# A multi-adapter linear layer and a mixture of low-rank experts: one index load, the bias sum on 64 partitions, and another order of the loads

## The reference

```python
# first layer, with one adapter pair per sequence, chosen by an index out of 32 slots
c = x @ W.T + b + 2.0 * (x @ A[idx]) @ Bm[idx]
# second layer
base = c @ W_base.T + b_base
logits = c @ W_router.T                    # 8 experts
rw, sel = top_k(logits, 2); rw = softmax(rw)
w = einsum('tk,tke->te', rw, one_hot(sel)) # weights of the experts per token
h = einsum('td,erd->ter', c, A_experts)    # rank 16 per expert
out = x + base + 2.0 * einsum('ter,te,eor->to', h, w, B_experts)
```

## Time and profile before

| | us |
|---|---|
| median of 3 runs | 67.73 |
| lowest and highest run | 66.97, 67.77 |
| the profiled execution's own time | 67.57 |
| its span | 65.8 |

### The profile page before, as it was taken

The page is one execution under the profiler, slowest core; times in us unless marked ns, Lnnn a source line. Parts: engine busy times, 40 slices in busy tenths (PEclk is TensorE's granted clock), DMA queues, the critical chain, the costliest instruction groups (busy, mean ns, idle before and its releaser), DMA issues.

```text
span 65.8 us, 1181 instructions
## 1 busy us (share of the span) xinstructions
PE 61.9 (94%) x424; PEld 60.8 (92%) x424; DVE 35.9 (55%) x103; ACT 21.5 (33%) x46; POOL 17.0 (26%) x30
## 2 busy tenths in 40 slices
PE   5999979999999999999999999999999999999930
PEld 5979879999999999998999999999999999999920
DVE  0056289998599667015935495002668363857320
ACT  0660358905989399127104100010201040020000
POOL 6810000000699982695390000010100000000000
PEclk9999999999999999999999999999999999999999
DMA  0899998219999004245559999700044000013532
GB/s 0 247 376 259 393 411 262 71 54 175 217 356 369 25 0 101 60 104 129 123 136 339 275 283 401 267 15 0 0 159 159 10 0 0 0 66 123 215 146 87
DMA packets 5865, 10.55 MB, mean 160 GB/s; under 512 B 731, under 2 KB 2523, under 8 KB 5860
## 3 DMA queue, kind: packets, MB, share of 16 engines
q1 hardware_dynamic: 5570, 10.15, 48.0%
q10 hardware_dynamic: 290, 0.33, 1.5%
HBM read 7.37 MB, written 2.10 MB: 144 GB/s over the span
## 4 chain that ended last, share of the span: by engine, by line
PE 83%; DMA 9%; SPq 1%; ACT 1%; DVE 1%; issue 1%
PE ps L661 26%; PE ps L673 19%; PE ps L567 17%; DMA wt<-w_chunks 9%; PE ps L721 9%; PE ps L628 5%; PE ps L696 2%; PE ps L701 2%; PE ps L684 1%; PE ps L707 1%; SPq L223 1%; ACT wt_hi L330 1%; PE ps L639 1%; DVE xn L520 1%
## 5 line engine op out<-in xcount | busy, mean ns | idle before, releaser
L661 PE MATMUL ps<-am,x_hi 128*128 128x384 f32 x64 | 16.6, 340 | 0.0
L673 PE MATMUL ps<-bm,x_hi 128*128 128x280 f32 x64 | 13.0, 297 | 0.0
L661 PEld LDWEIGHTS ps<-am,x_hi 128*128 128x128 f32 x64 | 11.4, 188 | 0.0
L661 PE MATMUL ps<-am,x_lo 128*128 128x384 f32 x32 | 10.8, 338 | 0.0
L297 POOL TENSOR_TENSOR x_lo<-xt,x_hi 128x512 fp32r<-128x512 f32 x8 | 10.8, 1367 | 0.0
L673 PEld LDWEIGHTS ps<-bm,x_hi 128*128 128x128 f32 x64 | 10.2, 188 | 0.0
L673 PE MATMUL ps<-bm,x_lo 128*128 128x280 f32 x32 | 9.3, 291 | 0.0
L567 PE MATMUL ps<-wt_hi 128*128 128x280 f32 (+1 forms) x32 | 7.4, 327 | 0.5 <-ACT wt_hi L330 0.3
L520 DVE TENSOR_TENSOR xn<-ps,xn 128x280 f32<-128x280 f32 (+1 forms) x16 | 6.1, 418 | 2.4 <-PE ps L721 2.3
L567 PE MATMUL ps<-wt_lo,wt_hi 128*128 128x280 f32 (+1 forms) x32 | 7.0, 316 | 0.0
L567 PE MATMUL ps<-wt_hi,wt_lo 128*128 128x280 f32 (+1 forms) x32 | 6.5, 310 | 0.0
(11 more groups left out here) (70 smaller groups left out, 98.5 us busy)
## 6 DMA issues: line engine op xcount, KB each, us to landing
xt<-x_t SPq DMA_DIRECT2D x4, 512.0 KB, 6.5
xn<-x_n SPq DMA_DIRECT2D x4, 512.0 KB, 6.0
out_n<-xn SPq DMA_DIRECT2D x7, 256.0 KB, 2.0
wt<-w_chunks SPq DMA_DIRECT2D x3, 582.0 KB, 6.6
g_st<-g_hl SPq DMA_DIRECT2D x12, 81.0 KB, 2.1
ab<-adapters SPq DMA_DIRECT2D x8, 64.0 KB, 2.7
wt<-w_chunks SPq DMA_DIRECT2D x2, 128.0 KB, 2.9
btt<-b_t SPq DMA_DIRECT2D x1, 256.0 KB, 5.0
```

The source lines that it names most:

```text
L661: last = mm(a_bank(b)[:, 0:R + WA], v[:, p, i, tok], am[:, i, level, at:at + R + WA], start=(i == 0 and n == 0), stop=False, skip_group_ch ...
L673: mm(b_bank(b)[:, 0:QB], v[:, p, i, tok], bm[:, i, level, :], start=(i == 0 and n == 0), stop=False, skip_group_check=True)
```

## The change

- `bsum` is not cleared, and `b_base` is not put into it. Its first step is a scaled copy of chunk 0's columns on ScalarE; VectorE adds the chunks 1 to 3.
- VectorE copies partitions 64 to 127 of `bsum` into a scratch that is the later `hw`, and adds them to partitions 0 to 63. ScalarE rounds these into the lower half of `bsum_st`; VectorE writes the low part into the upper half. `C` is then one matmul over 128 rows for each column range.
- `b_base` is the last of the loads, into one partition of the scratch. It is rounded into high and low parts of its own (`bb_hl`), which become two more rows of `g_st`: `GK` is 100 instead of 98, and `slots_routed(0)` waits for four spread rows instead of two.
- SP issues chunks 1 to 3 one after the other, then loads all eight indices with one call, then the adapters, then x's first pair and the rest.
- ScalarE rounds the adapters before x's first pair. POOL starts its series after `bsum_lo_done` instead of `bs_lo_done`. VectorE takes the low part of the bias sum before it reads `M` out.

The core of the diff:

```diff
-GK = CROW + 2
+GK = CROW + 4
...
+        bsum_st = sb("bsum_st", [P, WC], F32R)
+        cb_hl = sb("cb_hl", [HP + 1, 2, WC], F32R)
+        c_hl, bb_hl = cb_hl[0:1], cb_hl[HP:HP + 1]
...
+        hw_flat = hw[:].rearrange("p a t c -> p (a t c)")
+        upper, bb = hw_flat[0:HP, 0:WC], hw_flat[HP:HP + 1, 0:WC]
...
                 sp.dma_start(wt[:, k, :], w[:, k, :]).then_inc(w_in[k], 16)
-                if k == 1:
-                    sp.wait_ge(bsum_zero, 1)
-                    sp.dma_start(bsum[0:1, :], bbase).then_inc(bbase_in, 16)
-            sp.dma_start(xt[:, 0], x[:, 0]).then_inc(x_in[0], 16)
-
             sp.wait_ge(idx_in, 16)
-            for b in range(NB):
-                slot = sp.value_load(idx_sb[0:1, b:b + 1], min_val=0, max_val=SLOTS - 1)
+            _, slots = nc.values_load_multi_w_load_instructions(
+                idx_sb[0:1, :], engines=[mybir.EngineType.SP], min_val=0, max_val=SLOTS - 1)
+            for b, slot in enumerate(slots):
                 sp.dma_start(ab[:, b].rearrange("p c k r -> p (c k r)"),
...
+            sp.dma_start(xt[:, 0], x[:, 0]).then_inc(x_in[0], 16)
             sp.dma_start(xt[:, 1], x[:, 1]).then_inc(x_in[1], 16)
...
                 sp.dma_start(xt[:, p], x[:, p]).then_inc(x_in[p], 16)
+            sp.dma_start(bb, bbase).then_inc(bbase_in, 16)
+
+            def spread(row, src):
+                sp.dma_start(g_st[row:row + 1, :, :].bitcast(F32),
+                             src.bitcast(F32).to_broadcast([1, PAIRS, WC])).then_inc(cst_in, 16)
+
+            sp.wait_ge(bb_hi_done, 1)
+            spread(CROW, bb_hl[:, 0:1, :])
+            sp.wait_ge(bb_lo_done, 1)
+            spread(CROW + 1, bb_hl[:, 1:2, :])
...
-            nc.gpsimd.memset(bsum[:], 0.0).then_inc(bsum_zero, 1)
...
-            pool.wait_ge(bs_lo_done, 1)
+            pool.wait_ge(bsum_lo_done, 1)
             pool.wait_ge(ab_hi_done, 2)
...
+            act.wait_ge(w0_in[2], 16)
+            nc.scalar.activation(bsum[:], wt[:, 0, D:CH], ACT.Copy,
+                                 scale=wt[:, 0, CH:CH + 1]).then_inc(bsum_first, 1)
...
-            x_high(0)
             act.wait_ge(ab_in, 16 * NB)
             hi(bs_hi[:].rearrange("p k b r -> p b k r"), ab[:, :, 1]).then_inc(ab_hi_done, 1)
             hi(as_hl[:, :, :, 0, :], ab[:, :, 0]).then_inc(ab_hi_done, 1)
-            act.wait_ge(bsum_done, KB)
-            hi(bsum_hl[:, 0], bsum[:]).then_inc(bsum_hi_done, 1)
-
+            x_high(0)
+            act.wait_ge(halves_done, 1)
+            hi(bsum_st[0:HP], bsum[0:HP]).then_inc(bsum_hi_done, 1)
             for i in range(KB):
...
+            act.wait_ge(bbase_in, 16)
+            hi(bb_hl[:, 0], bb).then_inc(bb_hi_done, 1)
             x_high(1)
...
-                if k == 1:
-                    dve.wait_ge(bbase_in, 16)
-                bias_sum(k - 1)
+                if k > 1:
+                    bias_sum(k - 1)
             bias_sum(KB - 1)
+            dve.wait_ge(bsum_done, KB - 1)
+            nc.vector.tensor_copy(upper, bsum[HP:P]).then_inc(upper_done, 1)
+            dve.wait_ge(upper_done, 1)
+            nc.vector.tensor_tensor(bsum[0:HP], bsum[0:HP], upper, ALU.add).then_inc(halves_done, 1)
             dve.wait_ge(ab_hi_done, 1)
             lo(bs_lo[:].rearrange("p k b r -> p b k r"), ab[:, :, 1],
                bs_hi[:].rearrange("p k b r -> p b k r")).then_inc(bs_lo_done, 1)
+            dve.wait_ge(bsum_hi_done, 1)
+            lo(bsum_st[HP:P], bsum[0:HP], bsum_st[0:HP]).then_inc(bsum_lo_done, 1)
 
             for i in range(KB):
-                if i == 2:
-                    dve.wait_ge(bsum_hi_done, 1)
-                    lo(bsum_hl[:, 1], bsum[:], bsum_hl[:, 0]).then_inc(bsum_lo_done, 1)
...
+            dve.wait_ge(bb_hi_done, 1)
+            lo(bb_hl[:, 1], bb, bb_hl[:, 0]).then_inc(bb_lo_done, 1)
             for s, c in enumerate(COLS):
...
             for s, c in enumerate(COLS):
-                for i in range(2):
-                    last = mm(ps[:, C_BANK + s, 0:c.stop - c.start], ones_r[:], bsum_hl[:, i, c],
-                              start=(i == 0), stop=(i == 1))
+                last = mm(ps[:, C_BANK + s, 0:c.stop - c.start], ones_r[:], bsum_st[:, c], start=True, stop=True)
             last.then_inc(c_done, 1)
...
-                    pe.wait_ge(cst_in, 32)
+                    pe.wait_ge(cst_in, 64)
```

More of the change, by code:

```diff
@@ L45 @@
 AHEAD = 4
+HP = P // 2
 CH = D + WC
@@ L99, in build @@
         bsum = sb("bsum", [P, WC])
-        bsum_hl = sb("bsum_hl", [P, 2, WC], F32R)
+        bsum_st = sb("bsum_st", [P, WC], F32R)
+        cb_hl = sb("cb_hl", [HP + 1, 2, WC], F32R)
+        c_hl, bb_hl = cb_hl[0:1], cb_hl[HP:HP + 1]
         h_stack = sb("h_stack", [P, PAIRS, 2 * HSTEP])
@@ L160, in build @@
         bbase_in = sem("bbase_in")
-        bsum_zero = sem("bsum_zero")
         const = sem("const")
@@ L185, in build @@
         m_lo_done = sem("m_lo_done")
+        bsum_first = sem("bsum_first")
         bsum_done = sem("bsum_done")
+        upper_done = sem("upper_done")
+        halves_done = sem("halves_done")
         bsum_hi_done = sem("bsum_hi_done")
@@ L191, in build @@
         g_lo_done = sem("g_lo_done")
+        bb_hi_done = sem("bb_hi_done")
+        bb_lo_done = sem("bb_lo_done")
         c_done = sem("c_done")
@@ L257, in _ @@
                     for i in range(2):
-                        sp.dma_start(g_st[CROW + i:CROW + i + 1, :, :].bitcast(F32),
-                                     bsum_hl[0:1, i:i + 1, :].bitcast(F32).to_broadcast([1, PAIRS, WC])
-                                     ).then_inc(cst_in, 16)
+                        spread(CROW + 2 + i, c_hl[:, i:i + 1, :])
             for p in range(PAIRS):
@@ L374, in _ @@
             for s, c in enumerate(COLS):
-                hi(bsum_hl[0:1, 0, c], ps[0:1, C_BANK + s, 0:c.stop - c.start]).then_inc(c_hi_done, 1)
+                hi(c_hl[0:1, 0, c], ps[0:1, C_BANK + s, 0:c.stop - c.start]).then_inc(c_hi_done, 1)
             x_high(2)
@@ L410, in bias_sum @@
             def bias_sum(k):
-                if k > 0:
-                    dve.wait_ge(bsum_done, k)
+                if k == 1:
+                    dve.wait_ge(bsum_first, 1)
+                else:
+                    dve.wait_ge(bsum_done, k - 1)
                 nc.vector.scalar_tensor_tensor(out=bsum[:], in0=wt[:, k, D:CH], scalar=wt[:, k, CH:CH + 1],
@@ L459, in _ @@
                 dve.wait_ge(c_hi_done, s + 1)
-                lo(bsum_hl[0:1, 1, c], ps[0:1, C_BANK + s, 0:c.stop - c.start],
-                   bsum_hl[0:1, 0, c]).then_inc(c_lo_done, 1)
+                lo(c_hl[0:1, 1, c], ps[0:1, C_BANK + s, 0:c.stop - c.start],
+                   c_hl[0:1, 0, c]).then_inc(c_lo_done, 1)
             dve.wait_ge(bt_hi_done, 1)
```

## The result

The changed kernel took 68.50 us (median of 4 runs, 68.26 to 69.09), the kernel before 67.64 (4 runs, 66.97 to 67.77). The ratio is 1.018 (95% interval 1.011 to 1.025). In a second comparison on another chip it was 67.91 against 67.39, a ratio of 1.010 (1.006 to 1.013). So the change costs 0.5 to 0.9 us, and the prediction's 67.4, with its range of 66.7 to 68.1, misses the first result.

What follows compares the result with a forecast made beforehand. TensorE, busy 61.9 of 65.8 us, was taken to bound the kernel. Two matmuls fewer gave -0.30, all else hidden: span 65.5, 67.27 for the profiled execution, plus 0.16 for the median, 67.4 us; range 66.7 to 68.1.

Steps and rivals of the forecast that it cites:

- Index load, SP queue: SP's queue: one index load and eight adapter issues take 5.1 us (3.2 to 7.1), x's first pair issued at 9.7.
- rival (c): ScalarE, before G: x's first pair lands beyond about 15.4 us, each us costs one; 68.5 to 70.3 us; chance 0.11.
- Sum: Whole kernel: span 65.8 - 0.30 = 65.5 us, 67.27 for the profiled execution, median 0.16 above it: 67.4.
- The bias row's two matmuls: TensorE: two matmuls instead of four, which took 0.60 us; 0.30 us off, on the path.
- The copy, the addition and the low part on VectorE: VectorE's new bias steps: about 0.50, 0.83 and 0.83 us; halves joined at 16.5, low part ending at 18.1.
- VectorE's first evacuation: VectorE reading out M: starts at 18.1 instead of 17.61, second ends at 19.0 against 19.21: no stall, 0.2 us cover.
- The gap before chunk 1: TensorE's 0.33 us idle in front of 8.62: taken as unchanged, gain 0, with the whole gap as the other bound.
- rival (b): TensorE's start: chunk 1 lands earlier, the 0.33 us gap closes, nothing new stalls; 67.1 us; chance 0.20.
- Rival (d): SP's queue: the single index load fails, adapters stay 1.1 us apart, x lands at 18.4; 70.4 us; chance 0.02.
- Rival (a): VectorE first at 21.3, so POOL's x subtraction takes 1.89 us and TensorE stalls 0.2 to 0.3; 67.7; chance 0.17.
- The last rows of the stack: b_base's rows before the slot product: landed by 29.4 us, before 30.12; 0.7 us of cover, unchanged.
- two covers for POOL: x's first low part before routed: ready at 22.6 against 23.07, cover 0.45 us; before, 1.4 (23.37 against 21.94).

Runs made afterwards that it cites:

- c0: The changed kernel once more, unedited, with a second profile, on another chip: 67.91 us against 67.39 for the kernel before, ratio 1.010.
- e7: The changed kernel with the bounds checks of the eight indices left out: 67.86 us against 67.39 for the kernel before, ratio 1.010.
- e3: The kernel before with the changed loads and their rounding order alone, old bias sum kept: 67.55 us against 67.52, ratio 1.002.
- e1: The changed kernel with x's first pair issued right behind chunk 3, before the index wait: 67.68 us against 67.52 for the kernel before, ratio 1.003.
- e2: The changed kernel with ScalarE rounding the bias sum before x's first pair: 67.91 us against 67.52 for the kernel before, ratio 1.005.
- e6: The changed kernel with the bias sum's low part between M's second and third quarter, POOL waiting for bs_lo_done: 67.74 us against 67.39 before, ratio 1.008.
- e4: The changed kernel with the loads and their rounding as before, b_base still last: 67.48 us against 67.52 for the kernel before, ratio 0.998.
- h4: e4 with e6's edit and two ScalarE instructions fewer (chunk 3 rounded in one, b_base's high part on VectorE): 68.02 us against 67.38 before, ratio 1.007.

## Why the prediction was wrong

**The step "Index load, SP queue" failed.** It put x's first issue at 9.7 us; it came at 11.48 and 11.52 (c0). The term that was mis-sized is the register work, of which it took half. Three terms were too small. The index row was there at 4.47, in the range of 3.4 to 4.6 that I gave. The load of eight values took 0.73 us, not "up to 0.49". The register work did not go with the separate loads: eight checks from 5.2 to 7.47 take 2.3 us, of which I had counted half of 3.9, 1.9. And the eight issues are 0.52 us apart (3.97 us together), not 0.34: each has some register work and a pause of its own. From the start of the load that makes 7.0 us against 5.1, near the 7.1 of my upper bound: register work and pauses together are 3.5 of the 3.9 us, nearly all instead of half. e7, without the checks, issued x at 9.55, which shows their price: about 2 us.

**In the first profile x also lands later than 4.9 us after its issue.** I had taken the shortest landing of the four. It was 5.62 us there and 4.74 in c0, and SP's own issue took 1.61 against 0.43 us. That this is the whole difference isn't shown: with issues of 0.42 to 0.43 us ScalarE began with x 4.43 us (e3) to 5.18 us (e7) after the issue. In the first profile and in those of c0, e1, e2, e3 and e6 one issue on SP that starts between 11.4 and 12.5 us takes 1.4 to 1.9 us, and which one it hits changes from execution to execution (x's first pair, its second, or `btt`); where it hits x's first pair, the gap is 2.30 us, otherwise 0.81. The page lists three transfers of instructions (16 KB each) on a queue of their own. In these six traces one of them starts within 0.15 us of the long issue's start and ends 0.2 to 0.4 us before it does (first profile: 11.43 to 12.72 beside 11.48 to 13.09). In e7, though, an issue of 1.20 us starts at 11.44 and that transfer only at 14.50. So it may be the cause, and is not shown to be.

**So rival (c) happened, with its mechanism.** It had the place (ScalarE, in order, ahead of the bias sum and all evacuations), the point from which it decides (15.4 us; the rows put it between 14.7 and 15.7, by when `M` ends), and the price (a us for a us: from 16.29 to 17.13 the gap grew by 1.5, of which 0.64 are `M` ending earlier in that execution, as c0's ended at 19.17 and the first one's at 18.53, so 0.85 for 0.84 us). At 16.5 us it said 68.5. I gave it 0.11, because I took the median term at each link where the sum of three low terms was 1.8 us low. What (c) did not say is that the two halves of the change use up the same cover: in the medians of the spans the loads alone cost nothing (e3), the bias half alone gains 0.4 us (e4), and both together are 0.2 us above the kernel before (c0). At x's rounding from 15.7 or 16.0 us the order on VectorE decides whether there is a gap (e3, e6); at 17.13 it would by the estimate above only make it smaller. The prediction priced the two in separate paragraphs, each against the full cover.

**The step "Sum" failed too.** It took the 1.77 us outside the span as fixed. They rose by 0.36 to 0.38 us in the changed kernel, which takes back the whole gain of the two matmuls. This is the larger part of the loss in the second comparison: 0.38 us of rest and 0.2 of span. In the first, four runs with spans from 66.1 to 67.0 made it 0.4 us of rest and about 0.5 of span; why its spans are longer than c0's is open; a long issue on x's first pair, as in its profile, would do it.

**What held.** The bias row's two matmuls took 0.29 us against 0.60 for four, and with the old loads the span fell by about that (65.7 to 65.3 in e4). The copy, the addition and the low part on VectorE took 0.49, 0.82 and 0.83 us against 0.50, 0.83 and 0.83. With x on time VectorE's first evacuation came at 18.21 (e1) and 18.15 (e4), against 18.1, but the 0.2 us of cover behind it was not there: TensorE's loads idled 0.19 and 0.75 us. The gap before chunk 1, rival (b), can't be judged: ScalarE began with that chunk at 5.90 in the first profile and at 7.67 in c0, of the same kernel. Its clause that nothing new stalls when chunk 1 is early does not hold in e4, where `M` ended 0.8 us earlier than before and `G` began only 0.05 us earlier. Rival (d) did not happen. Rival (a) did not either: `bb_lo` came when POOL's subtraction was under way, and it was VectorE that waited, 1.78 us for a low part that takes 0.83 in e2, where POOL is idle for most of it. POOL's next subtraction, at 24.19, then took 1.90 us instead of 1.30, but the first pair's was done by then. That agrees with the Trainium skill, SBUF — State Buffer, "Who interferes with whom": the engine that issues first goes on. The last rows of the stack came in time; the slot product's weight load waited 0.21 us, as before. (The prediction's two covers for POOL are not on one scale: 22.6 is held against 23.07, but 21.94 against 23.37; against 23.07 the cover before was 1.1 us and not 1.4.)

## What to carry to other kernels

Before a load is moved back in its queue, add up the whole queue in front of it at its upper terms (address and bounds work too), and ask what stands behind its first reader in an in-order engine: work with slack of its own turns into a stall there. Two edits that are each hidden by the same cover have to be priced together, since each can be free and their sum not. And a gain of a few tenths in the span is to be set against the time outside it, which a change can move as well.

## What the runs showed of the hardware that was not expected

- The time outside the span follows the number of ScalarE's instructions, down to ones of a single column: 1.75 to 1.78 us at 46, 2.01 and 2.07 at 47, 2.11 to 2.18 at 48, and is indifferent to 16 more semaphores, two more DMAs and two more instructions on VectorE. Only these three counts were tried, so whether it is a slope or a step near 47 is open.
- An issue of a DMA on SP can take 1.4 to 1.9 us instead of 0.43, and not on the same one in each execution.
- Eight checked indices loaded by one instruction still cost 3.0 us of SP's time (0.73 for the load, 2.3 for the checks) before the first DMA that uses one.
- VectorE and POOL hold each other up on one partition as on 128: a low part of 1x648 took 1.78 us beside POOL's subtractions and 0.83 without them (e2). A plain cast of 1x648 took 1.00 us there (h4), where one of 128x512 took 0.43; that POOL is the cause was not tried for the cast.
